# A pairwise bilinear recommender tower on one core: step orders written out, PSUM banks shared, bf16 pieces read in place, ScalarE helping with one-hots and copies

## The reference, cut to what matters

```python
e = jnp.stack([tbl_0[ids[:, 0]], ..., tbl_39[ids[:, 39]]], axis=1)     # 512 x 40 x 32
vi, vj = e[:, I], e[:, J]                                              # the 780 pairs i < j
z = jnp.einsum('bke,kef,bkf->bk', vi, W, vj)                           # 512 x 780
h = jnp.concatenate([z, dense_ctx], axis=1)                            # 512 x 796
h = jnp.maximum(h @ W_top1 + b_top1, 0.0)                              # 512 x 512
h = jnp.maximum(h @ W_top2 + b_top2, 0.0)                              # 512 x 256
y = h @ W_top3                                                         # 512 x 1
```

## Time and profile before

| | |
|---|---|
| timed executions, median | 213.25 us (212.27 to 213.72) |
| profiled execution | 213.69 us |
| its span | 211.8 us |
| mean granted clock of PE | 0.984 |
| PE busy | 179.5 us |
| DVE busy | 143.9 us |
| POOL busy | 123.2 us |
| ACT busy | 35.0 us |

### The profile page before, as it was taken

The page is one execution under the profiler, slowest core; times in us unless marked ns, Lnnn a source line. Parts: engine busy times, 40 slices in busy tenths (PEclk is TensorE's granted clock), DMA queues, the critical chain, the costliest instruction groups (busy, mean ns, idle before and its releaser), DMA issues.

```text
span 211.8 us, 3006 instructions
## 1 busy us (share of the span) xinstructions
PE 179.5 (85%) x1228; PEld 52.0 (25%) x1228; DVE 143.9 (68%) x137; ACT 35.0 (17%) x45; POOL 123.2 (58%) x121
## 2 busy tenths in 40 slices
PE   3228986999898988859869999989988999999895
PEld 1003342342121222121123222232211222223340
DVE  0064899888998999837994877647987667681501
ACT  3083164001001100110002101121003201110321
POOL 3778778777777777777777777777004444400000
PEclk9999999799999999997999999999999999999999
DMA  2759997110110000001100000000000000000000
GB/s 52 220 173 262 260 347 268 62 16 14 15 14 16 12 14 14 16 12 14 14 16 12 14 14 15 13 13 15 3 5 0 0 3 0 0 0 3 0 0 0
DMA packets 7878, 10.28 MB, mean 49 GB/s; under 512 B 2729, under 2 KB 5545, under 8 KB 7865
## 3 DMA queue, kind: packets, MB, share of 16 engines
q1 hardware_dynamic: 4280, 8.25, 13.0%
q0 software_dynamic: 3584, 1.84, 5.7%
HBM read 10.08 MB, written 0.00 MB: 48 GB/s over the span
## 4 chain that ended last, share of the span: by engine, by line
PE 40%; POOL 39%; issue 13%; DVE 4%; DMA 2%; ACT 0%; SPq 0%; DVEq 0%; POOLq 0%
POOL rows L404 38%; PE ring_ps L612 12%; PE spare_ps L636 10%; PE z_ps L629 10%; PE ring_ps L678 3%; DVE prod L352 3%; PE ring_ps L636 2%; DMA rows<-table,idx 1%; POOL prod L352 1%; DMA idx<-ids 1%; PE ring_ps L683 1%; PE spare_ps L594 1%; ACT copied L444 0%; DVE zt L531 0%; DVE y_sb L538 0%
## 5 line engine op out<-in xcount | busy, mean ns | idle before, releaser
L352 DVE TENSOR_TENSOR prod<-ring_ps,emb 128x1024 f32<-128x1024 f32 x95 | 111.8, 1219 | 31.8 <-issue 28.3
L404 POOL DMA_INDIRECT rows<-table,idx x112 | 111.2, 992 | 36.9 <-issue 33.8
L612 PE MATMUL ring_ps<-emb,wall 32*128 32x512 f32 (+1 forms) x400 | 64.4, 654 | 11.8 <-DVE prod L352 9.3
L629 PE MATMUL z_ps<-prod,consts_sb 128*32 128x512 f32 x400 | 53.9, 611 | 1.1 <-DVE prod L352 0.6
L612 PEld LDWEIGHTS ring_ps<-emb,wall 32*128 32x128 f32 (+1 forms) x400 | 18.1, 187 | 53.8 <-DVE prod L352 38.2
L352 POOL TENSOR_TENSOR prod<-copied,emb 128x1024 f32<-128x1024 f32 x5 | 11.8, 2360 | 24.4 <-ACT copied L444 24.4
L636 PE MATMUL spare_ps<-zt,w_sb 128*128 128x512 f32 x44 | 23.9, 637 | 1.1 <-DVE zt L531 0.9
L581 PE MATMUL spare_ps<-one_hot,pieces 125*32 125x512 bf16 x312 | 20.5, 422 | 2.5 <-DVE pieces L489 2.5
L501 DVE TENSOR_SCALAR one_hot<-ids,vocab 125x2048 bf16<-125x2048 f16 x26 | 18.5, 754 | 5.6 <-PE spare_ps L581 5.0
L629 PEld LDWEIGHTS z_ps<-prod,consts_sb 128*32 128x32 f32 x400 | 8.0, 109 | 38.2 <-DVE prod L352 28.0
L437 ACT ACTIVATE emb<-spare_ps 128x512 f32<-128x512 f32 x10 | 5.9, 593 | 54.4 <-PE spare_ps L594 43.8
(11 more groups left out here) (22 smaller groups left out, 41.1 us busy)
## 6 DMA issues: line engine op xcount, KB each, us to landing
rows<-table,idx POOLq DMA_INDIRECT x112, 2.4
w_sb<-w SPq DMA_DIRECT2D x1, 1792.0 KB
table<-hot_table SPq DMA_DIRECT2D x2, 500.0 KB
wall<-w_pairs SPq DMA_DIRECT2D x1, 640.0 KB, 11.4
table<-hot_table SPq DMA_DIRECT2D x1, 625.0 KB
wall<-w_pairs SPq DMA_DIRECT2D x1, 576.0 KB, 10.4
w_sb<-w SPq DMA_DIRECT2D x1, 512.0 KB
wall<-w_pairs SPq DMA_DIRECT2D x1, 512.0 KB
```

The source lines that it names most:

```text
L352: return eng.tensor_tensor(prod[:, o % RING_P].rearrange(shaped, b=BATCH), products.rearrange(shaped, b=BATCH), emb[:, slots:slots + 1, :] ...
L404: nc.gpsimd.indirect_dma_start(rows[:, k, c, r, :], None, tables[f], bass.IndirectOffsetOnAxis(ap=idx[:, c, f:f + 1], axis=0)).then_inc(ga ...
L612: mm = nc.tensor.matmul(ring(o)[:, r % 2 * BATCH:(r % 2 + 1) * BATCH], wall[own, g, :], emb[own, stream, :], start=True, stop=True)
L629: mm = nc.tensor.matmul(z_ps[DIM * g:DIM * (g + 1), :], sel[:, m, :], prod[:, t // 2 % RING_P, t % 2 * BATCH:(t % 2 + 1) * BATCH], start=m ...
```

## The change

The tables of the hot quads go over 128 partitions (`HOT_ROWS` = P, the last rows padded with zeros), with 8, 8 and 10 tiles as before. The first and second piece are no longer cast by ACT: they are the upper halves of the float32 words of `table` and `rest`, read with a stride of two. The spreaders are a 12 x 12 matrix that is broadcast as it is read. Four of the one-hots are made by ACT from two activations. Six more ops are copied by ACT to SBUF and then multiplied by DVE from there; POOL has six ops in place of five. Seven banks of PSUM are shared by all uses but `z_ps`, by a written list `BANKS`. The planner is gone: the orders of PE, DVE and ACT are written out as letters. Layer 1 is done in the parts (0, 1), (2, 3), (4,), the matmuls of a part one behind the other. `w1` and `w2` are loaded after the last lookup, and `ids` comes first in SP's queue in a packed layout.

```diff
-HOT_ROWS = 125
+HOT_ROWS = P
-HOT_TILES = [v // HOT_ROWS for v in HOT_VOCABS]
+HOT_TILES = [-(-v // HOT_ROWS) for v in HOT_VOCABS]
-RING_BANKS = 3
-RING_P = 6
-RING_ONE_HOT = 4
-RING_HOT = 2
-RING_COPY = 2
-POOL_OPS = [78, 82, 86, 90, 94]
-PARTS = [(0, 1, 2), (3, 4)]
+RING_BANKS = 7
+RING_P = 8
+RING_ONE_HOT = 6
+RING_TABLE = 3
+RING_HOT = 2
+RING_COPY = 4
+PARTS = [(0, 1), (2, 3), (4,)]
+TENSOR_ORDER = ("iilillllllllllmlltlllllmlslmmslmsllllltmmmsmmsmsmssmmmtsmsmssmssmsmsm11t1msmmssmsm1mssmtsmmsmssmmsms"
+                "smmstsmsm1m1mssmssm1mstmmsm1mssmssm11msmssm11mssmsms")
+BANKS = ("0240624120642042043153053153052042054315305315302654025025035103514531531513515305230510352035031053"
+         "25315301535024620402065035130652")
+VECTOR_ORDER = ("pppppppppppppppppppwpppwpwpwwwpwwpppwwwwwwwwwwwwwwwwwwwwwwwwwwwwwwwwwwwwwwwwwwwwwwwwwwwwwwwwwwwwawww"
+                "awwwwwwwawwwwawwwwawawwaawwwww")
+SCALAR_ORDER = "IIIoIoLoIIoLLLLzLzL11c1Lzcc1LczccLcczccccz"
+POOL_OPS = [76, 78, 84, 90, 92, 94]
+COPIED_OPS = [38, 54, 58, 65, 73, 88]
+SCALAR_ONE_HOTS = [4, 10, 11, 18]
...
+PE_STEPS = in_order(TENSOR_ORDER, {
+    "i": [("spread", h) for h in range(len(HOT_AT))],
+    "l": [("hot", step) for step in HOT_STEPS],
+    "t": [("turn", q) for q in GATHERED_AT],
+    "m": [("map", g) for g in range(len(GROUPS))],
+    "s": [("sum", b) for b in range(NOPS // 2 - 1)],
+    "1": [("layer1", (part, m)) for part in range(len(PARTS)) for m in range(M1)],
+})
...
+DVE_STEPS = in_order(VECTOR_ORDER, {
+    "p": [step for h in range(len(HOT_AT)) for step in [("rest", h), ("third", h)]
+          + [("one_hot", (h, t)) for t in range(HOT_TILES[h]) if FIRST_ONE_HOT[h] + t not in SCALAR_ONE_HOTS]],
+    "w": [("weight", o) for o in range(NOPS) if o not in POOL_OPS],
+    "a": [("save1", (part, m)) for part in range(1, len(PARTS)) for m in range(M1)],
+})
+ACT_STEPS = in_order(SCALAR_ORDER, {
+    "I": [("ids16", (h, half)) for h in range(len(HOT_AT)) for half in range(2)],
+    "o": [("one_hot", HOT_STEPS[n]) for n in SCALAR_ONE_HOTS],
+    "L": [("land", q) for q in LANDINGS],
+    "c": [("copy", o) for o in ALL_COPIED],
+    "z": [("save_z", k) for k in range(ZTILES - 1)],
+    "1": [("save1", (0, m)) for m in range(M1)],
+})
+def bank_users():
+    digits = [int(digit) for digit in BANKS]
+    banks, before, last = {}, {}, {}
+    for step in PE_STEPS + [("tail", m) for m in range(M1)]:
...
+        size = 2 if kind in ("spread", "map") else 1
+        uses = 2 if kind == "spread" else len(OPS_OF[what]) if kind == "map" else 1
+        banks[step] = [digits.pop(0) for _ in range(uses)]
+        own = [(i, bank) for i, low in enumerate(banks[step]) for bank in range(low, low + size)]
+        before[step] = list(dict.fromkeys(last[bank] for _, bank in own if bank in last))
+        for i, bank in own:
+            last[bank] = (step, i)
+    return banks, before
...
+        def first_piece(h):
+            halves = table[:, h % RING_TABLE, :width(h)].bitcast(BF16)
+            return halves.rearrange("v (n two) -> v n two", two=2)[:, :, 1]
...
+            sp.dma_start(idx[:].rearrange("p c f -> p (c f)"), ids).then_inc(ids_loaded, 16)
             sp.dma_start(ids_sb[:], hot_ids).then_inc(hot_ids_loaded, 16)
-            sp.dma_start(idx[:], ids.rearrange("(c p) f -> p c f", p=P)).then_inc(ids_loaded, 16)
-            sp.dma_start(spread_sb[:].rearrange("k f v -> k (f v)"), spreaders).then_inc(spread_loaded, 16)
             load_table(0)
+            sp.dma_start(spread_sb[:], spreaders).then_inc(spread_loaded, 16)
             sp.dma_start(vocab[:], vocab_rows).then_inc(vocab_loaded, 16)
             load_table(1)
...
             load_weights(2)
-            load_weights(3)
-            for h in range(RING_HOT, len(HOT_AT)):
-                load_table(h)
-            load_weights(4)
+            load_table(2)
+            for q in range(3, QUADS):
+                load_weights(q)
...
             sp.dma_start(ctx_sb[:], ctx_rows).then_inc(ctx_loaded, 16)
-            load_weights(5)
-            load_weights(6)
+            sp.wait_ge(one_hot_used, FIRST_ONE_HOT[-1])
             sp.dma_start(w1_sb[:], w1.rearrange("k p n -> p k n")).then_inc(mlp_loaded, 16)
             sp.dma_start(w2_sb[:], w2.rearrange("(k p) n -> p k n", p=P)).then_inc(mlp_loaded, 16)
-            for q in range(7, QUADS):
-                load_weights(q)
...
+            def make_one_hot(h, t):
+                n = FIRST_ONE_HOT[h] + t
...
+                nc.scalar.activation(distance[:], ids16[:, h].rearrange("p r b -> p (r b)"), ACT.Abs,
+                                     bias=vocab_column(h, t, -1)).then_inc(distance_done, 1)
+                act.wait_ge(distance_done, SCALAR_ONE_HOTS.index(n) + 1)
+                nc.scalar.activation(one_hot[:, n % RING_ONE_HOT, :], distance[:], ACT.Relu, bias=vocab[:, 4 * MAX_TILES:],
+                                     scale=-1.0).then_inc(one_hot_by_scalar, 1)
...
             def weight_op(o):
...
                 if o >= RING_P:
                     dve.wait_ge(summed, (o - RING_P) // 2 + 1)
-                multiply(nc.vector, o, ring(o)[:]).then_inc(weighted, 1)
+                if o in COPIED_OPS:
+                    dve.wait_ge(copied_ready, copies(o))
+                    multiply(nc.vector, o, copied_op(o)).then_inc(weighted, 1)
+                else:
+                    dve.wait_ge(mapped, o + 1)
+                    multiply(nc.vector, o, op_banks(o)).then_inc(weighted, 1)
```

More of the change, by code:

```diff
@@ new lines, in in_order @@
+def in_order(letters, queues):
+    order = [queues[letter].pop(0) for letter in letters]
+    assert not any(queues.values())
+    return order
+ALL_COPIED = sorted(POOL_OPS + COPIED_OPS)
+HOT_STEPS = [(h, t) for h in range(len(HOT_AT)) for t in range(HOT_TILES[h])]
+PE_STEPS = in_order(TENSOR_ORDER, {
[6 more added lines that the diff above has]
+})
@@ new lines @@
+LANDINGS = [HOT_AT[what[0]] if kind == "hot" else what for kind, what in PE_STEPS
+            if kind == "turn" or kind == "hot" and what[1] == 0]
+DVE_STEPS = in_order(VECTOR_ORDER, {
[4 more added lines that the diff above has]
+})
@@ new lines @@
+ACT_STEPS = in_order(SCALAR_ORDER, {
[10 more added lines that the diff above has]
+    for step in PE_STEPS + [("tail", m) for m in range(M1)]:
+        kind, what = step
+        if kind == "sum" or kind == "hot" and what[1]:
+            continue
+        size = 2 if kind in ("spread", "map") else 1
[5 more added lines that the diff above has]
+            last[bank] = (step, i)
+    assert not digits
+    return banks, before
@@ L329, in build, with bank, pair, op_banks @@
         stored = sem("stored")
[L331 to L340 removed]
+        banks, before = bank_users()
+        def bank(step):
+            low, = banks[step]
+            return ring_ps[:, low, :]
+        def pair(step, i):
+            return ring_ps[:, banks[step][i]:banks[step][i] + 2, :]
+        def op_banks(o):
+            g, half = OPS[o]
+            return pair(("map", g), half)
+        others = [i for i in range(RING_BANKS) if i not in [banks["tail", m][0] for m in range(M1)]]
+        h2_ps = [ring_ps[:, others[m], :] for m in range(M2)]
+        y_ps = ring_ps[0:1, others[M2], :]
+        def landings(q):
+            return LANDINGS.index(q) + 1
         def by_pool(o):
@@ L346, in by_vector, with copies, copied_op @@
             return o + 1 - by_pool(o)
+        def copies(o):
+            return sum(c <= o for c in ALL_COPIED)
+        def copied_op(o):
+            return copied[:, ALL_COPIED.index(o) % RING_COPY]
         def multiply(eng, o, products):
             slots, _ = GROUPS[OPS[o][0]]
-            shaped = "p (t b) -> p t b"
-            return eng.tensor_tensor(prod[:, o % RING_P].rearrange(shaped, b=BATCH), products.rearrange(shaped, b=BATCH),
+            return eng.tensor_tensor(prod[:, o % RING_P], products,
                                      emb[:, slots:slots + 1, :].to_broadcast([P, 2, BATCH]), ALU.mult)
@@ L638, in layer1 @@
                 return mm
-            for kind, what in pe_steps:
+            for kind, what in PE_STEPS:
                 if kind == "spread":
@@ L672, in _ @@
             for m in range(M1):
[L673 removed]
+                layer1(bank(("tail", m)), TAIL[1:], m, start=False).then_inc(lin_done, 1)
             for m in range(M2):
```

408 lines of the change are left out of this document (139 added, 269 removed).

## The result

The changed kernel takes 206.46 us (median of 4 runs, 205.91 to 208.31), the kernel before 213.2 on the same chip (median of 4, 212.27 to 213.72): a ratio of 0.970, with an interval of 0.963 to 0.978. It is faster by 3%, 1.5 us slower than the 205.0 forecast and inside the range of 200 to 209.5. The profiled execution took 206.84 with a span of 205.0, against 213.69 and 211.8 before.

A forecast was written before the change was run, and what follows sets the result against it. The 112 gathers on POOL were taken to gate PE up to its last turn, with PE's work behind: 151.8 + 31.6 + 3.6 + 16.5 = 203.5 of span, 8.3 less, so a time of 205.0; range 200 to 209.5.

The forecast's parts named there:

- The end: Behind the last turn: 31.6 of PE work, 3.6 of tail matmuls, 16.5 from last sum to end.
- T6: PE's turn of the last quad, quad 6; forecast at 151.8, with its rows landing at 151.7.
- The start: Full-width tables bring table 0 near 5 and the first look-up near 8.5; priced at nothing in the total.
- DVE's second interval: From the second turn to the third DVE bounds with 17 ops; third turn forecast near 72.5.
- the gate: Gathers' landings set PE's turns; work before quad 0's turn, not before 27, costs nothing.
- T0: PE's turn of quad 0, first of seven numbered by quad; forecast at 27, when its rows land.
- the room: Between turns: a quad lands each 19.97, PE needs 16.3 to 20.8, so only the last interval lacks room.
- rival C: PE's handoff to DVE with three bank pairs stays behind the sixth turn: + 3.7, 208.7; chance 0.16.
- the sizes on POOL: Gathers: 0.3 saved by fewer DVE one-hots, 0.4 lost per multiply from SBUF; quads 5 and 6 at 130.9, 151.7.
- Rival B: Gathers' early loss of 5.5 came from transfers, not DVE, and goes: 198.6, half of it 201.8; chance 0.14.
- the sign of the copies: DVE multiplies of ScalarE's copies in SBUF were priced as a cost, 0.4 to the gathers for each of five.
- Rival D: Each of five DVE multiplies from SBUF keeps a gather off for its own 1.22: 209.0; chance 0.08.

The follow-up runs named there:

- experiment 1: Changed kernel with two ScalarE casts of the third quad's ids moved ahead of its second and third one-hot: 203.14 us, 0.950 of the kernel before.
- experiment 3: Changed kernel with every multiply doing only the first 256 of 512 batch columns, work left out: 201.54 us, 0.948 of the kernel before.
- experiment 4: Changed kernel without ScalarE's six copies for DVE, which multiplies those ops from PSUM; POOL's copies stay: 211.95 us, 0.992 of the kernel before.
- experiment 5: Changed kernel with seven more ops (10 to 23) copied by ScalarE and multiplied by DVE from SBUF: 206.65 us, 0.972 of the kernel before.
- experiment 6: Changed kernel with each table loaded in two DMAs, of 125 and 3 rows: 212.36 us, 0.995 of the kernel before.

## Why the prediction was right and wrong

The number held; its main step did not, and that the number held is in good part luck.

*Right.* The end: 31.6 + 3.6 + 16.5 = 51.7 were forecast behind T6, 51.2 came, with 16.5 of it exact. PE runs through there, and it is where the whole gain lies: 7.9, of which 6.5 is less busy time, most of it steps that the written order has in front of the last turn (counted from the orders and traces; no run moves them back). The start: table 0 "near 5" (5.14), the first look-up at 8.5 (9.35), a ScalarE one-hot of 4 (2.00 + 2.00). DVE's second interval, T2 at 72.5 (72.24).

*Wrong: the gate.* "All of it lies in front of quad 0's turn, which can't start before 27, so it costs nothing" priced ScalarE's one-hots at nothing. Their size was right. What was missed is what stands behind them in ScalarE's order, the casts of the third quad's ids, and who waits for those: the first map, for its bank. 4.57 us of wait and the lower clock behind it made T0 31.4, and experiment 1 shows 3.9 of it at the very end. The 5 us of idle PE that the prediction put in front of T1 stood in front of the first map instead.

*Wrong: the room.* "A quad lands each 19.97, so only T5 to T6 has no room of its own" compared the gathers with PE's bare work (16.3 to 20.8). The intervals measured are 19.8, 21.0, 19.4, 20.4, 20.9, 20.8: with the handoff to DVE (T5 to T6 by PE's own work, 20.68 busy of 20.90) each takes about what a quad takes, or more. So nothing behind T0 is made good, in no interval, and T5 passed without waiting for rows, which the prediction had named as what would prove it wrong. The mechanism is that of rival C, the handoff with three pairs of banks, at another place: it was looked for behind T5, where 34.28 of 34.60 leave it nothing, and it cost its 5.0 between T0 and T6 (experiment 3). The forecast walked T1 to T2 so, but let T2 to T3 and T3 to T4 go at PE's pace (18.8 and 17.9; measured 19.4 and 20.4) and counted 12 multiplies for T4 to T5 (18.2; 20.9).

*Wrong: the sizes on POOL, mildly.* Quads 5 and 6 landed at 128.1 and 148.5, not 130.9 and 151.7. The loss fell from 5.49 to 3.59 us before 52 us (5.5 less 0.3 was forecast), and the five multiplies from SBUF cost 0.08 each, not 0.4. Rival B, by which that loss goes, had a third of it right in size, not in its reason: gathers that began within one of the six subtractions lost 3.2 us in the kernel before and 1.6 in after, which is most of the 1.9, and it is DVE's doing and not that of transfers. There was nothing for the gathers to release either.

*Wrong: the sign of the copies.* They were priced by their cost to the gathers alone. That cost fell into room that the gathers had, and what they bring, a bank free without DVE, was given no price; it is 3.6 to 5.2 us here (experiment 4).

The path that exists, T0 at 31.4 and 122.4 of intervals, ends at 153.8; the one that was forecast, the gathers, at 151.8. They lie so near since both take about 20 us a quad. The right number is therefore worth less than it looks: of two equal paths the wrong one was named, and experiment 1 finds 3.9 us where the prediction says there is nothing.

Rival D, the multiplies that hold the gathers in full, has the mechanism right and the size wrong. The prediction read 1.29 beside one subtraction and 0.08 beside another as two ends of a range. The first gather began 0.06 behind the subtraction's start (35.79 and 35.85) and was held for nearly all of it. The second began 0.13 before its subtraction and lost 0.08:

```profile
26.58 1.02 POOL L404 DMA_INDIRECT rows<-table,idx  x1 [0.30 <-issue]
26.71 1.21 DVE L489 TENSOR_TENSOR pieces<-rest,pieces 125x1024 bf16<-125x1024 f32 x1
```

Only what is left of the DVE instruction when the next gather starts is lost, less 0.13, and in the kernel after that is little: one gather beside such a multiply took 1.33 (at 127.64, within the multiply from 126.94 to 128.16), and none of the others after 51 us over 1.00. With the same five ops it came to 0.39 each in experiment 5 and, by the same sum, to 0.5 each in experiment 6, with single gathers of 1.93 and 1.99. The Trainium skill, SBUF — State Buffer (*SBUF: two separate sides*), has a VectorE instruction with two SBUF inputs and a GpSimd instruction that reads SBUF exclude each other, the first to start for the whole of its instruction. The runs agree where the multiply or subtraction was first: the gather ends 0.82 behind it. Where the gather was first they show nothing of it: the multiply from 55.01 in experiment 5, beside a gather from 54.25 to 55.19, took its 1.22.

## What to carry to other kernels

Before a transfer is called the gate, compare when it lands with when its consumer is ready for it, for each stage and by the consumer's pace *with* its handoffs; where both paces are equal, a delay at the very start comes out at the very end. An instruction that only frees a buffer is as much on the path as one that computes: in an engine's written order, look at what stands behind a long instruction that "has time". And a copy to an idle engine is priced by when it frees its source, not by what it takes. Where two engines exclude each other, lay the start times of both side by side before an average is taken: 0.08 and 1.29 were one rule at two alignments.
